# Column halves, deviations four deep and no loops in the context stage of a perceiver layer

## The reference

```python
x = x + xattn(layernorm(x), ctx, Wv, bv, Wt, bt)
    # v = xn @ Wv.T + bv; t = ctx @ Wt.T + bt; (v . t) / max(|v||t|, 1e-8)
x = x + attn(layernorm(x), ...)        # 16 heads of 16, values' own direction taken out
x = x + ffn(layernorm(x), ...)         # 14 experts, top 1, 256 -> 512 -> 256, exact gelu
```

## Time and profile before

| | |
|---|---|
| median of 3 runs | 500.67 us (498.14, 500.67, 501.09) |
| the profiled execution | 500.66 us |
| its span in the trace | 498.8 us |
| granted TensorE clock, mean | 0.998 |
| PE busy, DVE, ACT, POOL | 97%, 68%, 67%, 49% |

### The profile page before, as it was taken

The page is one execution under the profiler, slowest core; times in us unless marked ns, Lnnn a source line. Parts: engine busy times, 40 slices in busy tenths (PEclk is TensorE's granted clock), DMA queues, the critical chain, the costliest instruction groups (busy, mean ns, idle before and its releaser), DMA issues.

```text
span 498.8 us, 14061 instructions
## 1 busy us (share of the span) xinstructions
PE 483.6 (97%) x4316; PEld 387.8 (78%) x4317; DVE 337.0 (68%) x1024; ACT 332.5 (67%) x809; POOL 245.2 (49%) x430
## 2 busy tenths in 40 slices
PE   8999999998999999999999999989999999999995
PEld 6544444566888888888888888768989999999994
DVE  4577675657889989998998999988573333333331
ACT  3765565569998898889889988977354334334331
POOL 2468754344344465566646555552674333332332
PEclk9999999999999999999999999999999999999999
DMA  8989998500001222322231122156475766666620
GB/s 308 266 210 291 252 300 246 174 2 2 1 2 39 84 57 92 97 96 63 87 97 62 53 66 58 52 148 207 160 225 190 243 217 198 223 215 190 217 89 30
DMA packets 35361, 69.98 MB, mean 140 GB/s; under 512 B 6672, under 2 KB 22034, under 8 KB 35296
## 3 DMA queue, kind: packets, MB, share of 16 engines
q1 hardware_dynamic: 31456, 60.06, 40.9%
q0 software_dynamic: 3408, 8.85, 4.7%
q10 hardware_dynamic: 432, 0.26, 0.3%
HBM read 58.27 MB, written 11.48 MB: 140 GB/s over the span
## 4 chain that ended last, share of the span: by engine, by line
PE 64%; DVE 6%; issue 4%; ACT 3%; POOL 2%; POOLq 0%; ACTq 0%; DVEq 0%
PE psum L1532 12%; PE psum L1545 11%; PE psum L1459 9%; PE psum L1436 6%; PE psum L1423 6%; PE psum L1415 6%; PE psum L1383 5%; PE psum L1488 5%; PE psum L1282 5%; DVE arena L912 1%; POOL out L614 1%; POOL tok L528 1%; ACT arena L1145 0%; DVE smax L901 0%; ACT arena L1181 0%
## 5 line engine op out<-in xcount | busy, mean ns | idle before, releaser
L1532 PEld LDWEIGHTS psum<-arena,ring 128*128 128x128 f32 x624 | 75.5, 192 | 2.6 <-issue 0.6
L1532 PE MATMUL psum<-arena,ring 128*128 128x128 f32 x624 | 76.1, 275 | 0.5 <-issue 0.5
L1545 PE MATMUL psum<-w_s,arena 128*128 x312 | 73.8, 380 | 0.0
L1215 ACT ACTIVATE arena<-psum 128x256 f32<-128x256 f32 x39 | 15.0, 385 | 84.0 <-PE psum L1282 79.4
L1036 DVE SCALAR_TENSOR_TENSOR arena<-psum,slot_rec,arena 128x256 f32<-128x256 f32 x39 | 18.9, 484 | 71.7 <-PE psum L1545 71.4
L556 POOL TENSOR_TENSOR ov<-o_n,v_s 128x256 f32<-128x256 f32 x32 | 26.1, 817 | 77.8 <-DVE o_n L794 77.8
L1545 PEld LDWEIGHTS psum<-w_s,arena 128*128 128x128 f32 x312 | 56.4, 190 | 6.3
L1181 ACT ACTIVATE arena<-kT,head_mask 128x256 f32<-128x256 f32 x128 | 59.3, 531 | 0.0
L614 POOL DMA_INDIRECT out<-arena,token_of x39 | 39.8, 1022 | 19.3 <-POOL token_of L606 14.6
L901 DVE TENSOR_REDUCE smax<-psum 128x16 f32<-128x1024 f32 x32 | 39.2, 1224 | 12.6 <-PE psum L1436 12.6
L1221 ACT ACTIVATE arena<-psum,b_s 128x128 f32<-128x128 f32 x156 | 44.4, 375 | 3.5 <-PE psum L1532 2.2
(11 more groups left out here) (206 smaller groups left out, 1074.7 us busy)
## 6 DMA issues: line engine op xcount, KB each, us to landing
ring<-w SPq DMA_DIRECT2D x39, 512.0 KB
w_s<-ctxT SPq DMA_DIRECT2D x15, 768.0 KB, 10.0
w_s<-w SPq DMA_DIRECT2D x16, 448.0 KB, 3.6
slot_rec<-routed SPq DMA_DIRECT2D x39, 132.0 KB, 3.7
tok<-x SPq DMA_DIRECT2D x16, 256.0 KB, 9.0
w_s<-xT SPq DMA_DIRECT2D x12, 256.0 KB, 7.4
routed<-pad_rec SPq DMA_DIRECT2D x1, 1980.0 KB, 8.7
tok<-b SPq DMA_DIRECT2D x14, 128.0 KB, 3.1
```

The costliest lines, as they stand in the source:

```text
L1532: mm = pe.matmul(hid_bank(p)[:, f * P:(f + 1) * P], w1_s[:, r, c * F + f * P:c * F + (f + 1) * P], xgT[:, p, c * P:(c + 1) * P], start=c = ...
L1545: mm = pe.matmul(bank(2 + q, D), hidT[:, q, f * P:(f + 1) * P], w2_s[:, bass.ds(e * (FC * D) + f * D, D)], start=f == 0, stop=f == FC - 1)
```

## The change

Four parts. (1) From pair 4 on, t's first pass and v are issued as two matmuls of 64 columns each instead of one of 128. (2) `std_b` and its semaphores go from two to four deep, and `wvc_s` moves to make room. (3) SP writes the deviations of pair i + 1 in step i (before: of pair i) and reads those of pair i - 1 (before: i - 2). From step 7 on both stand ahead of the load of x for pair i + 3. (4) The four loops are laid out.

```diff
+SPREAD = 4
-        std_b = arena[:, 2048:2048 + 4 * P].rearrange("p (s j) -> p s j", s=2)
-        wvc_s = arena[:, 2048 + 4 * P:2048 + 4 * P + KC * H].rearrange("p (c h) -> p c h", c=KC)
+        std_b = arena[:, 2048:2048 + 8 * P].rearrange("p (s j) -> p s j", s=SPREAD)
+        wvc_s = arena[:, 3328:3328 + KC * H].rearrange("p (c h) -> p c h", c=KC)
...
-                if not turned(i - 2):
-                    spread_deviations(i - 2, k % 2)
+                if i >= TURNED + 3:
+                    spread_deviations(i - 1)
+                    if i + 1 < NB:
+                        write_deviations(i + 1)
                 for n in (i + 2,) if i < 4 else (i + 2, i + 3) if i == 4 else (i + 3,):
                     if n < NB:
                         load_x(n, n % 4)
-                if not turned(i):
-                    need(sp, s["a_std"], i - TURNED + 1)
-                    sp.dma_start(deviations[...], pair_std[...]).then_inc(std_out[k % 2], 16)
+                if TURNED < i < TURNED + 3:
+                    spread_deviations(i - 1)
+                if i == TURNED:
+                    write_deviations(TURNED)
+                if TURNED <= i < TURNED + 3:
+                    write_deviations(i + 1)
...
+            def write_deviations(n):
+                sp.wait_ge(s["a_std"], n - TURNED + 1)
+                sp.dma_start(deviations[bass.ds(n, 1)]..., pair_std[:, bass.ds(n * 2, 2)])\
+                    .then_inc(std_out[n % SPREAD], 16)
-            def spread_deviations(n, q):
-                need(sp, std_out[q], arrivals(n - TURNED, q, 2, 16))
-                need(sp, s["v_sbuf"], n - 1)
+            def spread_deviations(n):
+                q = n % SPREAD
+                sp.wait_ge(std_out[q], arrivals(n - TURNED, q, SPREAD, 16))
+                need(sp, s["v_sbuf"], n - SPREAD + 1)
...
-            run_steps(pool, context_step, -4, NB - 1, 6, 10)
+            lay_steps(context_step, -4, NB - 1)
-            run_steps(dve, context_step, -4, NB - 3, 6, 10)
+            lay_steps(context_step, -4, NB - 3)
-            run_steps(act, context_step, -1, NB, 4, 12)
+            lay_steps(context_step, -1, NB)
-            run_steps(pe, context_step, -1, NB, 8, 12)
+            lay_steps(context_step, -1, NB)
...
+                    halved = not (isinstance(t, int) and t < TURNED)
+                    def first_pass(b):
+                        moving = ctx_in_sb[:, k, b * 2 * SC:(b + 1) * 2 * SC]
+                        if not halved:
+                            pe.matmul(t_bank(p, b), wt_s[:, 0, :], moving, start=True, stop=False)
+                            return
+                        for h in (slice(0, RG), slice(RG, P)):
+                            pe.matmul(t_bank(p, b)[h, :], wt_s[:, 0, h], moving, start=True, stop=False)
...
                         if raw:
-                            mm = pe.matmul(bank(p, 2 * P), wvc_s[:, c, :], xT_s[:, k, ...], start=c == 0, stop=c == KC - 1)
+                            for h in (slice(0, RG), slice(RG, P)):
+                                mm = pe.matmul(bank(p, 2 * P)[h, :], wvc_s[:, c, h], xT_s[:, k, ...],
+                                               start=c == 0, stop=c == KC - 1)
```

More of the change, by code:

```diff
@@ L298, in build @@
         ctx_in = [sem(f"ctx_in{n}") for n in range(4)]
-        std_in = [sem(f"std_in{n}") for n in range(2)]
-        std_out = [sem(f"std_out{n}") for n in range(2)]
+        std_in = [sem(f"std_in{n}") for n in range(SPREAD)]
+        std_out = [sem(f"std_out{n}") for n in range(SPREAD)]
         rec_out = [sem(f"rec_out{n}") for n in range(RING)]
@@ L346, in load_tokens @@
                         .then_inc(ctx_in[k], 16)
-                def turned(n):
-                    return isinstance(n, int) and not TURNED <= n < NB
-                if not turned(i - 2):
-                    spread_deviations(i - 2, k % 2)
+                if i >= TURNED + 3:
+                    spread_deviations(i - 1)
+                    if i + 1 < NB:
+                        write_deviations(i + 1)
                 for n in (i + 2,) if i < 4 else (i + 2, i + 3) if i == 4 else (i + 3,):
@@ L353, in load_tokens @@
                         load_x(n, n % 4)
-                if not turned(i):
-                    need(sp, s["a_std"], i - TURNED + 1)
-                    sp.dma_start(deviations[bass.ds(i, 1)].rearrange("o p h -> (o p) h"), pair_std[:, bass.ds(i * 2, 2)])\
-                        .then_inc(std_out[k % 2], 16)
+                if TURNED < i < TURNED + 3:
[4 more added lines that the diff above has]
+                    write_deviations(i + 1)
                 if 8 <= i < 8 + RESTS // 2:
@@ L360, in load_tokens @@
                         sp.dma_start(to, source).then_inc(s["consts_in"], 16)
-            def spread_deviations(n, q):
-                need(sp, std_out[q], arrivals(n - TURNED, q, 2, 16))
-                need(sp, s["v_sbuf"], n - 1)
+            def write_deviations(n):
+                sp.wait_ge(s["a_std"], n - TURNED + 1)
+                sp.dma_start(deviations[bass.ds(n, 1)].rearrange("o p h -> (o p) h"), pair_std[:, bass.ds(n * 2, 2)])\
+                    .then_inc(std_out[n % SPREAD], 16)
[3 more added lines that the diff above has]
+                need(sp, s["v_sbuf"], n - SPREAD + 1)
                 sp.dma_start(std_b[:, q, :], deviations[bass.ds(n, 1)].rearrange("o p h -> o (p h)").broadcast_to([P, 2 * P]))\
@@ L368, in _ @@
                 load_tokens(i, i % 4)
-            for n in (NB - 2, NB - 1):
-                spread_deviations(n, n % 2)
+            spread_deviations(NB - 1)
             sp.wait_ge(s["consts_made"], CONSTS)
@@ L692, in context_step @@
                     need(dve, s["dots_psum"], v - 1)
-                    need(dve, std_in[p], arrivals(v - TURNED, p, 2, 16))
+                    r = (k + 1) % SPREAD
+                    need(dve, std_in[r], arrivals(v - TURNED, r, SPREAD, 16))
                     if isinstance(v, int) and v == TURNED:
@@ L696, in context_step @@
                     dve.scalar_tensor_tensor(vT[:, p, :].rearrange("f (h t) -> f h t", h=2),
-                                             std_b[:, p, :].rearrange("f (t h) -> f h t", h=2), xbs_s[:, :],
+                                             std_b[:, r, :].rearrange("f (t h) -> f h t", h=2), xbs_s[:, :],
                                              bank(p, 2 * P).rearrange("f (h t) -> f h t", h=2), ALU.mult, ALU.add)\
@@ L1302, in context_step @@
                     need(pe, s["t_sbuf"], t - 1)
-                    pe.matmul(t_bank(p, 0), wt_s[:, 0, :], ctx_in_sb[:, k, 0:2 * SC], start=True, stop=False)
+                    halved = not (isinstance(t, int) and t < TURNED)
[6 more added lines that the diff above has]
+                            pe.matmul(t_bank(p, b)[h, :], wt_s[:, 0, h], moving, start=True, stop=False)
+                    first_pass(0)
                     if isinstance(i, int) and i == 0:
                         pe.wait_ge(ctx_in[0], 16)
-                    pe.matmul(t_bank(p, 1), wt_s[:, 0, :], ctx_in_sb[:, k, 2 * SC:4 * SC], start=True, stop=False)
+                    first_pass(1)
                     if isinstance(i, int) and i == 0:
@@ L1323, in context_step @@
                         if raw:
-                            mm = pe.matmul(bank(p, 2 * P), wvc_s[:, c, :], xT_s[:, k, c * 2 * P:(c + 1) * 2 * P],
-                                           start=c == 0, stop=c == KC - 1)
+                            for h in (slice(0, RG), slice(RG, P)):
+                                mm = pe.matmul(bank(p, 2 * P)[h, :], wvc_s[:, c, h], xT_s[:, k, c * 2 * P:(c + 1) * 2 * P],
+                                               start=c == 0, stop=c == KC - 1)
                         else:
```

## The result

The changed kernel took 504.64 us (median of 16 runs, 501.17 to 508.19) against 499.49 us before (16 runs): ratio 1.0099, 95% interval 1.0078 to 1.012. It is 1% slower where I had forecast 0.3% faster (499.2 against 500.66 us). The profiled execution took 504.74 us, its span 502.9 us: 4.1 us more than the span before.

The account below looks back on a forecast made before the run. PE was taken as the bound, with a context-stage step of 5.94 us. Forecast: 500.66 - 1.66 (halves) - 0.83 (old stalls) + 1.0 (late x) = 499.2 us, loops 0; range 497.0 to 502.5.

Parts of the forecast that it names:

- The halves: PE's raw steps in the context stage: column halves save 0.204 us a step by fewer form changes, 1.66 us in all.
- step 4: First PE step with halves: its predecessor hides part of the saving, so 0.12 us less, between 0 and 0.20.
- step 14's entry: PE entering step 14 behind a 128*128 form: nothing saved, a new form change costs 0.10 us (0 to 0.20).
- leaving v: PE after v in steps 14 and 15: a new form change each, costing twice 0.20 us.
- The old stalls: PE's two losses while DVE waited for deviations: gone with earlier transfers, 0.67 + 0.16 = 0.83 us less (0 to 0.83).
- The loops: The four loops laid out: worth 0, from -0.2 to +0.2 us, hidden behind PE.
- The failed step: DVE's L667: x of pair 10, behind SP's wait, lands at 44.8 against deadline 43.8, costing 1.0 us (0 to 3.6).
- rival B: SP's queue: at 205 GB/s x of pair 10 lands 3.6 us late, outweighing the halves; 501.8 us, chance 0.22.
- So I count the stall once: Loads of x after pair 10 keep level: 5.8 us of transfer per step against PE's 5.74, so no further stall.
- Rival A: SP's queue: at 275 GB/s or more x of pair 10 lands in time at 43.8; 498.2 us, chance 0.25.
- C: Rival: the cosines' chain of 5.71 us, if 0.07 longer, takes half a microsecond of the gain; 499.7 us, chance 0.06.
- D: Rival: PE's halves overlap only in part, a quarter more per halved pair, 7.7 us more; 506 us, chance 0.02.

Follow-up runs that it names:

- e9: e3 with the seven large weight loads moved behind x of pair 15 in SP's order; 498.15 us against 499.47 for the kernel before.
- e10: The changed kernel with x of pair 9 alone issued ahead of the wait for pair 6's deviation; 504.47 us against 499.47 for the kernel before.
- e6: The kernel before with the four loops laid out and nothing else; 499.75 us against 499.26.
- e3: The changed kernel with x loads ahead of both deviation transfers, pair 6's write behind step 6's loads; 499.48 us against 499.8 for the kernel before.
- e4: The changed kernel with DVE's statistics of the coming x behind the cosines; 499.81 us against 499.8 for the kernel before.
- e7: The changed kernel with the edits of e3 and e4 together; 499.38 us against 499.26 for the kernel before.
- e8: The kernel before with the column halves and DVE's statistics of the coming x behind the cosines; 499.51 us against 499.26.
- e1: The kernel before with the column halves alone; 498.89 us against 499.8.
- e2: The changed kernel with whole-array matmuls in place of the column halves; 503.28 us against 499.8 for the kernel before.
- e5: The changed kernel with the write of pair 6's deviations moved behind the loads of step 6; 503.14 us against 499.26 for the kernel before.

## Why the prediction was wrong

- **The halves: right.** Steps of 5.74, each form's change as priced. The small ends came out at: step 4 -0.15 (forecast -0.12), step 14's entry +0.05 (0.10), leaving v +0.20 and +0.16 (twice 0.20). e9, with all waits out of the way, gained 2.38 us in the stage, where halves and old stalls together were put at 2.49. The 2.38 that the Trainium skill has for three column tiles ("TensorE: Matmul & The Clock Gate", section "Measured speedup vs the span model") can't be tested here, as no run has three; the 1.26 that I had worked out from it for a pair of halves doesn't hold, for a pair costs 0.86 like one full matmul.
- **The old stalls: right.** In the changed kernel no wait of DVE for deviations is left (e10 has one of 0.5 us, behind which PE lost nothing).
- **The loops: right**, nothing (e6).
- **The failed step: "Late by 1.0 us: that is a new stall (0 to 3.6)."** The mechanism was the right one, named with its place (SP standing to 31.3, DVE at L667), but it was mis-sized three times over, and it belonged to rival B. In place of the 1.0 us, waits for x cost PE 5.6 us: 2.5 and 1.36 us of gaps and 1.7 us of half clock.
  1. *The wrong x first.* I worked out x of pair 10, since that was in time by nothing before. x of pair 9 stands behind the same wait, 8 us later than before, and its deadline was never worked out. It landed 8.0 us after its issue (32.61), near 40.6, and was needed at about 37.4.
  2. *The transfer time.* I took 250 GB/s from 33.3 on, since the queue would start empty. xT and context of pair 6 and x of pair 9, 1.31 MB, landed 7.3 us after 33.3: 180 GB/s, below my lower end of 205. x of pair 10 in e10 landed 9.8 us after its issue at 37.15 (late by 3.4), where I had 7.5. The hole itself was lost transfer time: from 20 to 40 us the changed kernel moved 2.9 MB, the kernel before 4.2 MB. And the 180 is no steady rate: the bytes began to move in bulk at 36 to 37 us and not at 33.3 (shown below).
  3. *What a gap on PE starts.* I priced the gap by its length. Behind a gap of 2.5 us the clock went to half for 3.4 us, 1.7 us more. My range's 3.6 had no such term.
- **"So I count the stall once"** failed too: x of pair 15 made a second gap of 1.36 us, because large weights stand ahead of it, which I had left to rival B (e3 keeps that gap, e9, which moves the weights, has none).
- Rival B, given 0.22 and 501.8 us, was the case that came, 3 us short of the time. Rival A is excluded. C didn't hold the changed kernel, but stands 0.03 us below PE's step, and e4, e7 and e8 ran into it. A trace of it is in e9 too: the step of pair 6 took 5.85 us, with PE's L1301 starting 0.13 us late, right behind the cosines. D is excluded.
- By medians the change costs 5.15 us, by the two profiles 4.1. The profile of before I had worked from lay 1.2 us above the later median of 499.49: it took 6.4 us from the start of the last matmul to the end of the span, and the profile of e1, with the same code there, 4.4. In the twelve profiles this tail is 4.4 to 4.5 us in five (e1, e4, e6, e7, e9) and 5.9 to 6.6 in seven, so two spans can differ by 2 us with nothing changed in the context stage; that is why the stage's own end is given beside each median.

The windows behind point 2, of the changed kernel (first two lines) and of the one before (last two), with the columns as above:

```profile
33.00:36.00 3.00, 3.00 (x20) 1.00 0.40 38
37.00:41.00 4.00, 3.09 (x18) 1.00 1.05 379
33.00:36.00 3.00, 3.00 (x16) 1.00 1.18 95
37.00:41.00 4.00, 4.00 (x22) 1.00 1.10 398
```

Both have a slow stretch and then one well above my 250 GB/s (later, from 40 to 47 us, e10 moved 273). The queue of the kernel before hadn't run empty, for it moved 117 GB/s from 31 to 33 us, so the empty queue is not shown to be the cause of the slow stretch.

What stays open: why the queue moved so little from 33 to 36 us, in the changed kernel and in the one before, and some 380 to 400 GB/s from 37 on. No run here varied that alone. And the 1.5 us at the handover: in the profiles of the changed kernel, e2, e3, e4 and e5 the clock fell there, in those of before, e1 and e6 to e10 it didn't, at the same gap of 1.57 us. I know of no difference in code that sorts them. That it is chance of the single execution is a guess and not shown.

## What to carry to other kernels

When a wait moves up in a queue that works in order, work out the deadline of each transfer that now stands behind it, not only of the one that was tightest; the first one behind the wait was the costly one here. Put what other engines need soonest ahead of any wait for something that is made late, and large loads with slack last (e9). A form's change on PE can be counted from start to start, and here it paid as counted, but a gain of 0.2 us a step is worth having only if the next chain (here 5.71 against 5.74) and the transfers leave room for it.

## What the runs showed of the hardware

Two 64-column float32 matmuls, issued one behind the other with the same moving operand, cost 0.86 us as one of 128 columns does, so the first pass takes 1.71 us for both banks. Where the form changes between full and column halves, the group ahead costs 0.10 us more (the dots 0.97 against 0.86) and the group behind 0.10 more (t's first pass 0.96 against 0.86); ahead of row halves v costs 0.95 to 0.97, against 0.86 ahead of its own form. For two small groups (L1394, L1291) it was 0.06 to 0.07. The granted clock fell from full to half (2.4 to 1.2 GHz) for 3.4 us after gaps of 1.8, 2.5 and 3.0 us on PE in the context stage (e2, the changed kernel, e10), at a price of 1.7 us each time; after gaps of 0.7 to 1.3 us (e1, e3, e5, and the changed kernel's second) it didn't. At the handover the clock fell inside a gap of 1.57 us in five profiles and not in the other seven. From 33 to 36 us the DMA queue moved 38 GB/s in the changed kernel and 95 in the one before, from 37 to 41 us 379 and 398.
